# A four-layer cross-attention and FFN kernel: opening split between ScalarE and GpSimd, other PSUM banks for two norms, 3+3 turn pieces, shifted projections, and a token-by-token end

## The reference

```
x = x + L0_xattn(norm(x), ctx, ctx, mask)   # 32 query heads, 8 kv heads, 128 wide, rotary
x = x + L0_ffn(norm(x))                     # gated SiLU FFN
x = x + L1_xattn(norm(x), ctx)              # 16 heads, 4 kv heads, 96 wide, keys from ctx and x
x = x + L1_ffn(norm(x))                     # base product + sparsemax-routed LoRA
x = x + L2_xattn(norm(x), ctx)              # 32 heads, 4 kv heads, 128 wide, keys from ctx and x
x = x + L2_ffn(norm(x))                     # top-16 of 64 rank-16 experts
x = x + L3_xattn(norm(x), ctx, ctx, mask)   # 32 heads of 16, 8 kv groups
x = x + L3_ffn(norm(x))                     # two 8-bit linears (512 -> 2048 -> 512) with outlier columns in float
```

## Time and profile before

| | |
|---|---|
| median of three runs | 2056.43 us (2055.41 to 2062.31) |
| the profiled execution's own time | 2061.42 us |
| its span | 2059.6 us |
| mean granted clock of PE | 0.983 |
| PE, DVE, ACT, POOL busy | 1959.6, 1480.3, 1112.6, 843.1 us |

### The profile page before, as it was taken

One profiled execution on the slowest core, in us unless ns is written; L12 is line 12 of the kernel. 1 busy time (PEld: TensorE's weight loads), 2 busy tenths in 40 slices (PEclk: granted clock), 3 DMA queues, 4 the chain that ended last, 5 costly groups with the idle time before them and its releaser, 6 DMA issues.

```text
span 2059.6 us, 32190 instructions
## 1 busy us (share of the span) xinstructions
PE 1959.6 (95%) x11708; PEld 1662.0 (81%) x11716; DVE 1480.3 (72%) x2999; ACT 1112.6 (54%) x2315; POOL 843.1 (41%) x822
## 2 busy tenths in 40 slices
PE   6999999999899999988999999999998999998887
PEld 4888888888778888877888889889887877876665
DVE  6777777777676777666667767667676477777798
ACT  4756666566325555641556556555554167776333
POOL 6554654542633122043443253343215733151762
PEclk9999999999999999999999999999999999999899
DMA  4101111010213232012111121111111200120210
GB/s 154 52 22 52 52 41 43 21 52 21 90 29 81 74 91 56 23 39 72 42 44 55 42 67 55 41 67 60 43 47 41 99 23 22 42 83 1 71 57 21
DMA packets 49053, 107.56 MB, mean 52 GB/s; under 512 B 18560, under 2 KB 28032, under 8 KB 41600
## 3 DMA queue, kind: packets, MB, share of 16 engines
q1 hardware_dynamic: 35072, 84.51, 12.1%
q10 hardware_dynamic: 13824, 20.98, 3.3%
HBM read 97.08 MB, written 5.24 MB: 50 GB/s over the span
## 4 chain that ended last, share of the span: by engine, by line
PE 85%; DVE 8%; issue 2%; ACT 2%; POOL 2%; DMA 1%; SPq 0%; ACTq 0%; DVEq 0%; POOLq 0%
PE ps_s L326 11%; PE ps_s L328 11%; PE ps_s L327 11%; PE ps_t L1112 8%; PE ps_t L326 7%; PE ps_t L328 6%; PE ps_t L327 6%; PE ps_o L326 5%; PE ps_o L328 4%; PE ps_o L327 4%; PE ps_o L1854 3%; PE ps_t L1885 2%; PE ps_s L1840 2%; PE ps_t L1119 1%; DVE l_pt_lo L1240 1%
## 5 line engine op out<-in xcount | busy, mean ns | idle before, releaser
L1167 ACT ACTIVATE l_pt_hi<-ps_t 128x512 fp32r<-128x512 f32 (+1 forms) x512 | 244.7, 515 | 319.3 <-PE ps_t L1112 294.5
L1232 DVE TENSOR_REDUCE nmax<-ps_s 128x1 f32<-128x768 f32 x192 | 183.7, 957 | 232.3 <-PE ps_s L328 230.4
L1240 DVE TENSOR_TENSOR l_pt_lo<-ps_t,l_pt_hi 128x512 fp32r<-128x512 f32 (+1 forms) x512 | 281.6, 581 | 5.3 <-ACT l_pt_hi L1167 5.3
L1198 ACT ACTIVATE l_p<-ps_s,nmax 128x768 f32<-128x768 f32 x192 | 173.6, 904 | 150.3 <-DVE nmax L1232 149.6
L1112 PE MATMUL ps_t<-ident,l_p 128*128 128x128 f32 x1664 | 237.9, 274 | 10.6 <-DVE l_pt_lo L1240 5.2
L326 PE MATMUL ps_o<-l_pt_hi,l_v_hi 128*128 128x256 f32 (+1 forms) x832 | 236.8, 285 | 5.8 <-DVE l_pt_lo L1240 5.8
L1112 PEld LDWEIGHTS ps_t<-ident,l_p 128*128 128x128 f32 x1664 | 197.9, 141 | 53.3 <-issue 11.5
L328 PE MATMUL ps_o<-l_pt_hi,l_v_lo 128*128 128x256 f32 (+1 forms) x832 | 235.0, 282 | 0.0
L327 PE MATMUL ps_o<-l_pt_lo,l_v_hi 128*128 128x256 f32 (+1 forms) x832 | 234.6, 282 | 0.0
L326 PE MATMUL ps_s<-l_k_hi,l_q_hi 128*128 128x512 f32 (+3 forms) x512 | 206.7, 404 | 1.3 <-ACT l_p L1198 1.2
L364 POOL TENSOR_TENSOR wo_hi<-raw_big,one 128x512 fp32r<-128x512 f32 (+2 forms) x100 | 103.5, 1035 | 193.5 <-PE ps_t L328 181.7
(11 more groups left out here) (397 smaller groups left out, 5375.1 us busy)
## 6 DMA issues: line engine op xcount, KB each, us to landing
raw_big<-in_l_wq SPq DMA_DIRECT2D x18, 1024.0 KB, 4.8
raw_big<-in_l_wo SPq DMA_DIRECT2D x18, 1024.0 KB, 4.8
w_raw<-in_f_w ACTq DMA_DIRECT2D x32, 256.0 KB, 3.1
raw_big<-in_f_w SPq DMA_DIRECT2D x7, 1024.0 KB, 4.9
raw_kv<-in_l_wkv SPq DMA_DIRECT2D x12, 512.0 KB, 5.7
raw_f<-in_f_w SPq DMA_DIRECT2D x4, 1024.0 KB, 4.8
w_nat<-in_f_w1n ACTq DMA_DIRECT2D x16, 256.0 KB, 3.0
w_nat<-in_f_w2n ACTq DMA_DIRECT2D x16, 256.0 KB, 3.0
```

Source lines behind the costliest of these rows:

```text
L1167: e.activation(sp.pt[u % 2][0][:, k0:k0 + nk, qt * P:(qt + 1) * P], ps_t[p % 2][:, 0:nk * P].rearrange("p (k q) -> p k q", q=P), ACT.Copy) ...
L1198: e.activation(sp.p[:, k % 3, :], sp.p[:, k % 3, :] if l.rope else self.scores_out(k), ACT.Exp, bias=nmax[:, i:i + 1], scale=-1.0 if l.rop ...
L1232: e.tensor_reduce(nmax[:, i:i + 1], self.scores_out(k), AX.X, ALU.max, negate=True).then_inc(s_max, 1)
L1240: e.tensor_tensor(pt[1], ps_t[p % 2][:, 0:nk * P].rearrange("p (k q) -> p k q", q=P), pt[0].bitcast(F32), ALU.subtract).then_inc(s_tlo, 1)
```

## The change

1. **Opening.** The high parts of the first kv weight and the first query weight are written by ACT (`first_hi`), POOL writes only the low parts (`first_lo`). ACT's order becomes: kv high parts, context 0, query high parts, context 1, and only then the turned x. POOL makes all four kv low parts, then `rstd` of norm 0, then the query low parts.
2. **Banks of norm 0.** Its turned x goes to ring[0], ring[1], ring[2] and ps_t[0]. So v0, in ps_t[2], no longer waits for the turned x; the wait moves to job 2 (q0), part by part. The kv jobs wait for their weight and context part by part.
3. **Turn pieces of layers 1 and 2**: three and three blocks in place of four and two.
4. **Fills.** In the first group of layer 1, K1 goes from slot 4 to slots 2,2,3,3 and V1 from slot 6 to 4,4,6,6; in that of layer 2, q3 from slot 2 to 2,2,3,3.
5. **Norm 7 in halves.** Statistics of token tiles 0 and 1 on DVE at the end of slot 117 of layer 3, their `rstd` on POOL at the end of slot 118, their scaling on DVE at the start of slot 122. PE turns token tile by token tile into ring[1], ring[2], ring[3] and one of ps_t[0], ps_t[1]; `out_bank` is ordered so that the last FFN's first job takes the other one.
6. **End.** Blocks 0 to 11 of the last product stay as they were; blocks 12 to 15 run token tile by token tile.

```diff
-        self.pieces = [(0, 4), (4, 2)] if self_keys else [(0, 4)]
+        self.pieces = [(0, 3), (3, 3)] if self_keys else [(0, 4)]
...
+        def first_hi(act, role, n, cols):
+            act.wait_ge(w_in[role], 16 * n + 16)
+            for piece in range(4):
+                act.activation(W[role][0][:, piece, 0:cols], RAW[role][:, piece, 0:cols], ACT.Copy).then_inc(s_fhi, 1)
+        def first_lo(pool, role, done, cols):
+            for piece in range(4):
+                pool.wait_ge(s_fhi, done + piece + 1)
+                pool.tensor_tensor(W[role][1][:, piece, 0:cols], RAW[role][:, piece, 0:cols],
+                                   W[role][0][:, piece, 0:cols].bitcast(F32), ALU.subtract).then_inc(w_rdy[role], 2)
...
-                self.halves = i in (1, 3, 5)
-                self.banks = [ring[0], ring[1], ring[2], ps_t[0][:, :]] if self.halves else turn_banks
+                self.halves = i in (1, 3, 5, 7)
+                self.banks = last_norm_banks if i == 7 else [ring[0], ring[1], ring[2], ps_t[0][:, :]] if self.halves or i == 0 else turn_banks
...
-            "l1": "q0@-3 K0@-2 q1@-1 q2@0 V0@1 K1@4 V1@6 "
+            "l1": "q0@-3 K0@-2 q1@-1 q2@0 V0@1 K1@2,2,3,3 V1@4,4,6,6 "
...
-            "l2": "q0@-3 K0@-2 q1@-1 q2@0 V0@1 q3@2 K1@4 V1@6 "
+            "l2": "q0@-3 K0@-2 q1@-1 q2@0 V0@1 q3@2,2,3,3 K1@4 V1@6 "
...
                     elif part == 0 and j.n == 1:
-                        e.wait_ge(s_xout, TT)
                         if c.g:
                             e.wait_ge(g_free, c.g)
...
+                    if j.n == 2 and not c.g:
+                        e.wait_ge(s_xout, part + 1)
...
-                        if part == 0:
-                            e.wait_ge(w_rdy["kv"], 8 * (c.kv + j.g + 1))
-                            e.wait_ge(s_csplit[j.i], DK)
+                        e.wait_ge(w_rdy["kv"], 8 * (c.kv + j.g) + 2 * part + 2)
+                        e.wait_ge(s_csplit[j.i], part + 1)
...
+                if k == 118:
+                    norms[7].pool_half(e, 0)
...
+                if k == 122:
+                    norms[7].dve_scale(e, 0)
...
+                if k == 117:
+                    e.wait_ge(s3["job_out"], find3["o", 2, 1].n + 1)
+                    norms[7].dve_stats(e, link, 0)
...
+        last_turn = piece_at3["t", N3 - 1] % 2
+        last_norm_banks = [ring[1], ring[2], ring[3], ps_t[last_turn][:, :]]
...
+            for hb in range(HT - 4):
                 for t in range(TT):
+                    int_second(hb, t)
+            for t in range(TT):
+                for hb in range(HT - 4, HT):
+                    int_second(hb, t)
...
-            for piece in range(2):
-                split(e, "kv", a0.c.kv, None, piece, cols=256)
+            first_lo(e, "kv", 0, 256)
             norms[0].pool(e)
-            for piece in range(2, 4):
-                split(e, "kv", a0.c.kv, None, piece, cols=256)
-            split_all(e, "q", a0.c.q, None)
+            first_lo(e, "q", 4, 512)
...
+            first_hi(e, "kv", a0.c.kv, 256)
             for b in range(B):
                 ...
                 if b == 0:
-                    norms[0].act(e)
+                    first_hi(e, "q", a0.c.q, 512)
+            norms[0].act(e)
```

More of the change, by code:

```diff
@@ L244, in program @@
         s_chi = sem("context_hi")
+        s_fhi = sem("first_weights_hi")
         s_ve = sem("var_eps_ready")
@@ L403, in dve @@
                     self.dve_scale(e, 1)
-                    turn_dve(e, self.c.g, self.c.hi, xT, self.banks)
+                    if self.i == 7:
+                        f3_norm_dve(e, link)
+                    else:
+                        turn_dve(e, self.c.g, self.c.hi, xT, self.banks)
                     return
@@ L422, in dve, with pool_half @@
                         e.wait_ge(s_xhi, d + 1)
-                        e.tensor_tensor(xT[1][:, d, :], turn_banks[d][:, :], xT[0][:, d, :].bitcast(F32),
+                        e.tensor_tensor(xT[1][:, d, :], self.banks[d], xT[0][:, d, :].bitcast(F32),
                                         ALU.subtract).then_inc(s_xout, 1)
-                elif self.i == 7:
-                    f3_norm_dve(e, link)
                 else:
                     turn_dve(e, self.c.g, self.c.hi, xT, self.banks)
+            def pool_half(self, e, half):
+                e.wait_ge(s_ve, 2 * self.i + half + 1)
+                c = slice(2 * half, 2 * half + 2)
+                e.tensor_tensor(rstd[:, c], veps[:, c], mhalf[:, c], ALU.pow).then_inc(s_rstd, 1)
             def pool(self, e):
                 if self.halves:
[L432 to L435, removed]
+                    for half in range(1 if self.i == 7 else 0, 2):
+                        self.pool_half(e, half)
                 else:
@@ L454, in pe @@
                         for t in range(TT):
-                            mm = e.transpose(turn_banks[d][:, t * P:(t + 1) * P], xn[:, t, d * P:(d + 1) * P], ident[:, :])
+                            mm = e.transpose(self.banks[d][:, t * P:(t + 1) * P], xn[:, t, d * P:(d + 1) * P], ident[:, :])
                         mm.then_inc(s_xfull, 1)
@@ L463, in act @@
                         e.wait_ge(s_xfull, d + 1)
-                        e.activation(xT[0][:, d, :], turn_banks[d][:, :], ACT.Copy).then_inc(s_xhi, 1)
+                        e.activation(xT[0][:, d, :], self.banks[d], ACT.Copy).then_inc(s_xhi, 1)
                 elif self.i == 7:
@@ L2081, in f3_pool @@
                 e.tensor_tensor(x[:, t, :], x[:, t, :], q_c[:, t, :], ALU.add).then_inc(s4["added"], 1)
-        out_bank = [ps_t[0][:, :], ps_t[1][:, :]]
+        out_bank = [ps_t[1 - piece_at3["t", N3 - 1] % 2][:, :], ps_t[piece_at3["t", N3 - 1] % 2][:, :]]
         int_bank = [ps_t[2][:, :], ps_o[:, :]]
         acc_i = [ps_t[0][:, :], ps_t[1][:, :], ps_t[2][:, :], ps_o[:, :]]
+        last_turn = piece_at3["t", N3 - 1] % 2
+        last_norm_banks = [ring[1], ring[2], ring[3], ps_t[last_turn][:, :]]
         def f3_norm_act(e):
@@ L2092, in f3_norm_act @@
                 e.wait_ge(g_full, cf.g - 4 + d + 1)
-                e.activation(xF[:, d, :], turn_banks[d][:, :], ACT.Copy).then_inc(s4["x_kept"], 1)
+                e.activation(xF[:, d, :], last_norm_banks[d], ACT.Copy).then_inc(s4["x_kept"], 1)
                 if d:
@@ L2185, in f3_pe, with int_second @@
             e.wait_ge(s_wback[1], 16)
-            for hb in range(HT):
+            def int_second(hb, t):
                 if hb in DVE_TILES:
@@ L2190, in f3_pe @@
                     e.wait_ge(s4["h_int"], hb + 1 - sum(p < hb for p in DVE_TILES))
+                mm = e.matmul(acc_i[t], hq[:, hb, t * P:(t + 1) * P], q_w2[:, hb, :], start=hb == 0, stop=hb == HT - 1)
+                if hb == HT - 1:
+                    mm.then_inc(s4["acc"], 1)
+            for hb in range(HT - 4):
                 for t in range(TT):
-                    mm = e.matmul(acc_i[t], hq[:, hb, t * P:(t + 1) * P], q_w2[:, hb, :], start=hb == 0, stop=hb == HT - 1)
-                    if hb == HT - 1:
-                        mm.then_inc(s4["acc"], 1)
+                    int_second(hb, t)
+            for t in range(TT):
+                for hb in range(HT - 4, HT):
+                    int_second(hb, t)
         def f3_act(e):
```

## The result

The changed kernel takes 2046.62 us (median of 5 runs, 2043.72 to 2050.9), the kernel before 2056.43 in the runs shown ahead. Timed beside each other, the ratio is 0.9942, 95% interval 0.9929 to 0.9955: 11.9 us less, between 9.3 and 14.6. Forecast were 2045.2 us and -11.2.

A forecast was written before the change was run, and what follows sets the result against it. PE, busy for 95% of the span, was taken as the bound, so only its stops and the ends could give time. -6.0 - 1.8 - 0.3 - 1.4 - 1.7 = -11.2 took 2056.43 to 2045.2 us; 8 in 10 within 2039 to 2052.

The forecast's parts named there:

- Opening, -6.0: Start of the kernel: earlier k0, v0 without its stop and shorter POOL queue bring q2 6.0 us sooner, carried on.
- xn beside POOL: Opening: DVE's four xn scalings each can wait for a POOL low part; xn done at 17.5 us.
- the row's upper price: DVE's scaling of one tile: 1.18 us beside a busy POOL, against 0.48 beside an idle one.
- Fills, -1.8: First slots of layers 1 and 2: moved projections fill stops and advance work, -1.0 and -0.8 us.
- fill the first stop: Layer 1, tile 3's scores: two parts of K1, 0.72 us, moved into PE's 1.21 us stop.
- Pieces, -0.3: Turns of layers 1 and 2: 3+3 blocks gain only where a drain exposes latency, -0.3 us (+4 to -3).
- The rival in which 3+3 holds PE: Turns: each of 192 tiles waits up to 0.13 us, 2070 us in all; decides from 0.06 a tile; 5%.
- Norm 7, -1.4: Last norm: 1.9 us saved behind the last addition, 0.5 paid earlier; -1.4 us (-2.2 to +0.5).
- The charge of 0.5: Late layer 3: DVE's inserted work delays low parts PE waits for, charged 0.5 us (0 to 1.5).
- End, -1.7: Behind the last matmuls: tiles complete one after another, so DVE's last addition ends 1.7 us sooner (-1.0 to -2.0).
- The clock rival (20%): Opening: level rises only after turns and v0, which pay 4.3 us; opening -2, sum -7, 2049.2 us; 20%.
- The sum, -11.2: Whole kernel: opening, fills, pieces, last norm and end add to -11.2 us, giving 2045.2 us.

The follow-up runs named there:

- e8: Kernel before with only ACT's high parts of the first weights, ACT's new order and waits part by part; old turn banks: 2055.25 us, ratio 0.9984.
- e9: Kernel before with only norm 0's new banks and v0 freed from its wait; old POOL and ACT order: 2060.26 us, ratio 1.0011.
- e1: Kernel before with only the new opening and norm 0's new banks: 2051.98 us, ratio 0.9966 to the kernel before.
- e10: Changed kernel with 3+3 pieces in layer 1, 4+2 in layer 2, norm 0's turns token tile by token tile: 2048.2 us, ratio 0.9947 to the kernel before.
- e12: The kernel of e10 with the old fills of layers 1 and 2: 2049.71 us, ratio 0.9955 to the kernel before.
- e4: Kernel before with only the turn pieces of three and three blocks: 2057.73 us, ratio 0.9995.
- e6: Kernel before with only the last four blocks run token tile by token tile: 2056.59 us, ratio 0.9987.
- e5: Kernel before with only norm 7 in halves: 2059.81 us, ratio 1.0003.
- e11: The kernel of e10 without the halves of norm 7: 2047.83 us, ratio 0.9946 to the kernel before.

## Why the prediction was right

- **Opening, -6.0.** Right at every start that it named: k0 11.08 (11.0 forecast), xn done 17.48 (17.5), q0 22.38 (22.3), q2 28.44 (28.1), scores 33.88 (33.6). Alone it measured -7.0 us. e8 and e9 show what it rests on: v0's wait and, behind it, the bank that ACT's old order held; POOL's and ACT's orders were changed together and v0's wait beside them, and the sum comes only when all go. Behind k0 the idle time was 1.79 us for the forecast 1.2, since the level rose inside k0 (its matmuls stand 0.23 us apart from 14.63 on) and k0 was through at 15.74, not 16.3; xn decided all the same. Not forecast was that a half-level stretch may come behind any of the short stops here: at 17 us in e1, 22 in e8, 28 in e9, 54 in the kernel before, nowhere in the first 100 us of the changed kernel.
- **xn beside POOL.** xn took 4.82 us for four tiles beside the query low parts, 1.2 each in the mean, the row's upper price. The mean hides what happened: the first tile began before POOL's first query low part and took 0.54 us, the other three took 1.5 each and ended 0.29 us behind the end of one low part each (14.34, 15.78, 17.19 us). So POOL's queue set the end of xn. By the Trainium skill's page on "SBUF — State Buffer", in its section on the two separate sides, VectorE and GpSimd share a port pair that one instruction holds to its end. The trace agrees, and more sharply in the drain: an operation on 128x2 waited for the rest of POOL's instruction (1.11 us; 0.17 without).
- **Fills, -1.8.** The size agrees with the runs (-1.9, -3.9 to +0.2), which can't tell it from none; the traces give about 1 us, and the reason was wrong. The step that failed is that parts of K1 and V1 "fill the first stop" and cost nothing where they left: I never asked what they had covered in slots 3 to 7. The stops of layer 1 grew from 2.86 to 3.82 us (before against after, those of 0.5 us and more). What the runs show in its place is the granted clock behind the fill. In layer 1 this made 0.5 us in the mean of the traces (0.87 for 0.35), where 1.0 was forecast. Layer 2's fill gave nothing in itself: e10 and e12 leave it with the lead they had, within 0.2 us. But of the eight kernels with the old fills four (e1, e4, e6, e9) lost 1.0 to 1.1 us there to a half-level stretch of 3.4 us at 987 to 994 us, and of the six with the new ones none; four of eight against none of six may be chance.
- **Pieces, -0.3.** Right in sum. The rival in which 3+3 holds PE exists at a tenth of its threshold: 1.0 us over 192 tiles, 0.005 us a tile, between the turns of one tile. The drain pays it back, most of it by the order in which `veps` and POOL's low part come.
- **Norm 7, -1.4.** From the start of layer 3's last addition on x to the end of DVE's last addition of all, the six kernels with old norm 7 and old end take 153.2 to 154.3 us, mean 153.8, e5 151.6; with the new end e6 and e11 take 151.7 and 152.0, the five with the halves 149.65 to 150.1. That is -2.0 to -2.2, and the new stop in slot 122 takes 0.7 back: -1.3 to -1.5 in the traces. A part of it may be the clock: around this norm five of the six kernels with the halves have 6.8 us at the half level (the changed kernel 10.2), six of the eight without have 13.7 (the other two 10.2). The charge of 0.5 was measured as 0.68. But neither e5's runs (+0.6, -1.4 to +2.5) nor e11 (0.2 us faster than e10 by the ratios, each uncertain by 3) show a gain. In e5's trace half-level stretches in layer 3, ahead of the edit, hide it: 13.7 us for the 6.8 before. Whether norm 7 pays in the mean stays open.
- **End, -1.7.** Right: -1.6 between the same two events, -1.8 to -2.0 by the sums just given, -2.7 (-4.7 to -0.6) in the runs.
- **The clock rival (20%)** did not come as told. It let the level rise only behind the turns and v0. In every opening with k0 near 11 us the turns or the last part of k0 already run at the full level. What came instead, in e1, was a fall back to the half level at the turns, which cost 1.5 us, not 4.3. By the Trainium skill ("TensorE: Matmul & The Clock Gate", part 1) the throttled level is the default; the openings agree in so far as k0's first matmuls stand 0.43 us apart in every one, and do not say when the level drops again.
- **The sum, -11.2.** It came within 0.7 us of the measured -11.9, and a part of that is luck. Measured alone the parts are -7.0 (opening), -1.0 (pieces), -1.9 (fills), +0.6 (norm 7) and -2.7 (end), each uncertain by 2 to 3 us. Opening and end, 7.7 of the 11.2, are borne out in time and in mechanism. The fills gained by another way than forecast, the pieces are two unforeseen effects that cancel, and norm 7 is not shown in the runs.

## What to carry to other kernels

Waits in a row on one path must be removed together: measured alone, one looked worth half of what it brings, and the other like a loss. Before moving work into a stop, look at what it covers where it stands; the sum of the stops may grow. For effects of 1 to 2 us in 2050, compare the time between two named events in many traces rather than whole runs, since the stretches at the half level move the whole by as much.

## What the hardware showed that I had not expected

- A DVE operation on two columns took 1.11 us instead of 0.17 because a POOL instruction of 1.26 us had begun 0.17 us before it, in eight kernels of eight.
- A POOL power of 128x2 took 0.69 us, of 128x4 1.01 or 1.02: halving it saves a third.
- The granted clock reads 1.00 at 11 to 14.6 us, where k0's matmuls stand 0.43 us apart; they stand 0.23 apart from 14.63 on. The trace's first clock record is at 14.67 us (20.11 in the kernel before), so the 1.00 ahead of it is no measurement. At the start of the program the spacing is the better clock.
- The time at the half level summed to between 49.9 and 79.9 us in the profiled executions of kernels that differ by 0.7%, up to 15 us of PE time and more than any part of the change.
